# Half of the first normed rows made by ScalarE, and four of the last eight combines put ahead of the last sums

## What is computed

```python
x = x + attn_a(layernorm(x), Wv, Wg, Win, Wout, ...)   # gated, groups of 32, quadratic part and running kv sum
x = x + ffn(layernorm(x), Wr, W1, b1, W2, b2)          # 8 experts, top 2, capacity 160 per batch
x = x + attn_b(layernorm(x), q_w, k_w, v_w, l_w, ...)  # 16 heads of 64, softmax over the query axis
x = x + ffn(layernorm(x), Wr, W1, b1, W2, b2)

def layernorm(x, eps=1e-5):
    return (x - mean(x)) / sqrt(var(x) + eps)

# in ffn, for each token and each of its two experts
y_tok = y[e_flat, b_idx, pos_c] * keep * p_flat        # the answer of the slot that the token got
out = y_tok.reshape(B, T, K, C).sum(axis=2)            # its two answers are summed
```

## Time and profile before

| | |
|---|---|
| plain runs, median of 3 | 1536.02 us (1535.35 to 1537.2) |
| profiled execution, its own time | 1544.41 us |
| span of the profiled execution | 1542.6 us |
| PE busy | 1456.9 us (94%) |
| DVE, ACT, POOL busy | 1068.5 (69%), 918.2 (60%), 282.6 us (18%) |
| chain that ended last, by engine | PE 81%, DVE 9%, ACT 5% |

### The profile page before, as it was taken

One profiled execution on the slowest core, in us unless ns is written; L12 is line 12 of the kernel. 1 busy time (PEld: TensorE's weight loads), 2 busy tenths in 40 slices (PEclk: granted clock), 3 DMA queues, 4 the chain that ended last, 5 costly groups with the idle time before them and its releaser, 6 DMA issues.

```text
span 1542.6 us, 43235 instructions
## 1 busy us (share of the span) xinstructions
PE 1456.9 (94%) x18426; PEld 1010.9 (66%) x18426; DVE 1068.5 (69%) x2176; ACT 918.2 (60%) x1723; POOL 282.6 (18%) x325
## 2 busy tenths in 40 slices
PE   6999889999999999999999999999999999999956
PEld 5889774465677755657777556577775565775746
DVE  7875047787766678876666788766667887777632
ACT  4665566555666656556666566566665656666512
POOL 4156523413000031030000311300003013000170
PEclk9999999999999999999999999999999999999987
DMA  7501221111000010010000101100001011000011
GB/s 219 185 18 47 71 62 35 43 28 44 16 16 16 16 52 23 21 45 16 15 16 16 53 23 34 45 16 15 16 16 53 22 36 43 15 19 12 2 38 35
DMA packets 44302, 58.29 MB, mean 38 GB/s; under 512 B 8199, under 2 KB 32624, under 8 KB 43984
## 3 DMA queue, kind: packets, MB, share of 16 engines
q1 hardware_dynamic: 34960, 38.27, 8.9%
q0 software_dynamic: 9152, 17.26, 4.0%
HBM read 22.14 MB, written 19.32 MB: 27 GB/s over the span
## 4 chain that ended last, share of the span: by engine, by line
PE 81%; DVE 9%; ACT 5%; another core or an unknown queue 3%; issue 2%; DMA 0%; DVEq 0%; ACTq 0%; SPq 0%
PE bank L1075 28%; PE bank L1088 24%; PE bank L1003 5%; DVE nmx L1110 4%; PE bank L1008 3%; PE bank L1017 3%; PE bank L401 3%; PE bank L373 2%; ACT prob L1119 2%; PE bank L1230 2%; PE bank L1226 2%; PE bank L1187 1%; ACT hT L495 1%; PE bank L774 1%
## 5 line engine op out<-in xcount | busy, mean ns | idle before, releaser
L1119 ACT ACTIVATE prob<-bank,nmx 128x1024 f32<-128x1024 f32 x512 | 570.2, 1114 | 440.7 <-DVE nmx L1110 439.4
L1110 DVE TENSOR_REDUCE nmx<-bank 128x1 f32<-128x1024 f32 x512 | 625.8, 1223 | 211.0 <-PE bank L1075 195.8
L1088 PE MATMUL bank<-prob,vsc 64*64 64x512 f32 x4096 | 643.4, 590 | 4.7 <-DVE ctxT L1137 3.0
L1075 PE MATMUL bank<-q,k 64*64 64x512 f32 x2048 | 531.7, 593 | 14.5 <-ACT prob L1119 13.2
L1075 PE MATMUL bank<-q,ks 64*64 64x512 f32 x2048 | 529.1, 592 | 0.0
L1088 PEld LDWEIGHTS bank<-prob,vsc 64*64 64x64 f32 x4096 | 233.7, 133 | 130.2 <-issue 63.5
L1003 PE MATMUL bank<-xT,wqkv_sb 64*64 64x256 f32 (+1 forms) x1560 | 211.7, 434 | 0.0
L1075 PEld LDWEIGHTS bank<-q,ks 64*64 64x64 f32 x2048 | 135.7, 132 | 85.1 <-issue 24.2
L1647 POOL DMA_INDIRECT yg<-yslots,row_ring x64 | 65.1, 1017 | 587.1 <-PE bank L1075 571.7
L1075 PEld LDWEIGHTS bank<-q,k 64*64 64x64 f32 x2048 | 133.2, 133 | 53.9 <-ACT prob L1119 27.6
L1003 PEld LDWEIGHTS bank<-xT,wqkv_sb 64*64 64x64 f32 x1560 | 91.8, 133 | 87.7 <-issue 32.2
(11 more groups left out here) (264 smaller groups left out, 1646.1 us busy)
## 6 DMA issues: line engine op xcount, KB each, us to landing
ks<-k SPq DMA_DIRECT2D x64, 256.0 KB
yslots<-slots_sb SPq DMA_DIRECT2D x7, 640.0 KB, 3.6
slots_sb<-xslots SPq DMA_DIRECT2D x5, 640.0 KB, 4.5
xslots<-xhat_r POOLq DMA_DIRECT2D x5, 512.0 KB, 7.1
yslots<-xhat_r POOLq DMA_DIRECT2D x5, 512.0 KB, 12.2
w_sb<-in_w SPq DMA_DIRECT2D x1, 2048.0 KB, 9.4
wqkv_sb<-in_wqkv SPq DMA_DIRECT2D x1, 2048.0 KB, 18.8
xslots<-xhat_r,row_s POOLq DMA_INDIRECT x112
```

The source lines that it names most:

```text
L1075: ins = nc.tensor.matmul(bank[rows(c), SC[h][n], :], kk[r, cols(2 * j + c, HD)], qst[pi % 2][r, cols(n, HALF)], start=True, stop=True)
L1088: ins = nc.tensor.matmul(bank[rows(h), CX[n], :], vsc[s][rows(r), rows(h)], prob[g % 3][h][rows(r), cols(n, HALF)], start=(j == 0 and firs ...
L1110: nc.vector.tensor_reduce(nmx[:, 2 * s + h:2 * s + h + 1], bank[:, SC[h][0]:SC[h][0] + 2, :], mybir.AxisListType.XY, ALU.max, negate=True) ...
L1119: nc.scalar.activation(prob[g % 3][h][:].rearrange("p (n c) -> p n c", c=HALF), bank[:, SC[h][0]:SC[h][0] + 2, :], ACT.Exp, bias=nmx[:, 2 ...
```

## The change

In the head, DVE makes a `shift` for tiles 4 to 7 only (four columns) and raises `la_warm`; then it makes tiles 0 to 3 and raises `la_xhat` by two. ACT waits for `la_warm` and makes tiles 4 to 7, then raises `la_half`. PE's second turn and POOL's bias of row 0 wait for `la_half` besides. In the tail, DVE does the first four combines of k = 1 ahead of the sums, and the other four behind them; the last four gathers count on a semaphore of their own, `g_late`. SP stores the first half of batch 2 ahead of the two stores of batch 3.

```diff
--- before.py
+++ after.py
@@ bias_gpsimd
             xb = xres[:, row * T:(row + 1) * T, :]
+            if row == 0:
+                p.wait_ge(la_half, 1)
             p.wait_ge(la_xhat, 2 * (row + 1))
@@ a_turn_tensor
                 pe.wait_ge(la_xhat, 2 * row + h + 1)
+                if row == 0 and h == 1:
+                    pe.wait_ge(la_half, 1)
                 half_turned(xhat, h, bk + h).then_inc(la_tr, 1)
@@ xhat_vector
-        def xhat_vector(v, c0, b, xh, half, done):
+        def xhat_vector(v, c0, b, xh, half, done, count=1):
...
-            ins.then_inc(done, 1)
+            ins.then_inc(done, count)
@@ f_combine_vector
-            v.wait_ge(g_ga[k], 16 * T * b)
+            if b < B or k == 0:
+                v.wait_ge(g_ga[k], 16 * T * b)
+            elif tiles[0] == 0:
+                v.wait_ge(g_ga[k], 16 * (T * b - T // 2))
+            else:
+                v.wait_ge(g_late, 16 * (T // 2))
@@ sync engine
+        def store_third(sp, h):
+
+            hold(sp, g_comb, 2 * T * B - 4 * (1 - h))
+            r = slice((B - 2) * S + h * HALF, (B - 2) * S + (h + 1) * HALF)
+            sp.dma_start(out[r, :].rearrange("(t p) c -> p t c", p=P),
+                         xres[:, (B - 2) * T + 4 * h:(B - 2) * T + 4 * h + 4, :]).then_inc(stored, 16)
@@ c_gather
-                                                 bounds_check=B * SLOTS - 1, oob_is_err=False).then_inc(ga[k], 16)
+                                                 bounds_check=B * SLOTS - 1, oob_is_err=False).then_inc(
+                                                     g_late if b == B and k == 1 and t >= T // 2 else ga[k], 16)
@@ sync engine, at the end
             for h in range(2):
+                if h == 0:
+                    store_third(sp, 0)
                 hold(sp, t_res, 2 * (h + 1))
...
-            for h in range(2):
-                hold(sp, g_comb, 2 * T * B - 4 * (1 - h))
...
+            store_third(sp, 1)
             sp.wait_ge(stored, 16 * (B + 2))
@@ scalar engine, at the start
             nc.scalar.activation(wa_hi[:], wa_sb[:], ACT.Copy).then_inc(a_split, 1)
+            a.wait_ge(la_warm, 1)
+            xhat_scalar(N_MAIN[0], 0, xhat, 1, la_half)
             a.wait_ge(consts, 1)
@@ vector engine, at the start
-            for half in range(2):
-                xhat_vector(v, N_MAIN[0], 0, xhat, half, la_xhat)
+            shift_vector(v, step, N_MAIN[0] + 4, la_warm, 4)
+            xhat_vector(v, N_MAIN[0], 0, xhat, 0, la_xhat, 2)
@@ vector engine, at the end
             answers_vector(v, [2])
+            f_combine_vector(v, step, B, 1, range(T // 2))
             sums_vector(v)
-            f_combine_vector(v, step, B, 1, range(T))
+            f_combine_vector(v, step, B, 1, range(T // 2, T))
```

More of the change, by code:

```diff
@@ L154, in bass_hybrid @@
         g_ga = [sem("g_ga0"), sem("g_ga1")]
+        g_late = sem("g_late")
+        la_warm, la_half = sem("la_warm"), sem("la_half")
         t_hi, t_lo, t_oh = sem("t_hi"), sem("t_lo"), sem("t_oh")
@@ L1888, in _ @@
                              xres[:, (B - 1) * T + 4 * h:(B - 1) * T + 4 * h + 4, :]).then_inc(stored, 16)
-            for h in range(2):
-                hold(sp, g_comb, 2 * T * B - 4 * (1 - h))
-                r = slice((B - 2) * S + h * HALF, (B - 2) * S + (h + 1) * HALF)
-                sp.dma_start(out[r, :].rearrange("(t p) c -> p t c", p=P),
-                             xres[:, (B - 2) * T + 4 * h:(B - 2) * T + 4 * h + 4, :]).then_inc(stored, 16)
+            store_third(sp, 1)
             sp.wait_ge(stored, 16 * (B + 2))
```

## The result

| | before | changed |
|---|---|---|
| runs, median | 1536.83 us (1533.33 to 1539.1, 20 runs) | 1534.86 us (1532.28 to 1537.01, 20 runs) |
| profiled execution, its own time | 1544.41 us | 1535.34 us |
| its span | 1542.6 us | 1533.6 us |
| PE busy in it | 1456.9 us (94%) | 1452.4 us (95%) |

The ratio is 0.9988, with a 95% interval of 0.9983 to 0.9994: 1.8 us faster, 0.9 to 2.6. That lies above nothing and within the 0.2% that the prediction calls no change.

A forecast was written before the change was run, and what follows sets the result against it. PE, 94% busy, was taken to bound the kernel except at its two ends, where chains of waits count. Head 0.7 plus tail 1.05 gave 1.75 us off the 1536.02 median: 1534.3 us, range 1531.9 to 1537.3.

The forecast's parts named there:

- DVE's first half: Head, row 0: with the shift ahead costing 0.1 us, DVE's four tiles end at about 9.97 instead of 9.86.
- ACT's four tiles: Head, row 0: ACT makes tiles 4 to 7 in 1.64 us, unblocked by POOL, ready at 10.6 instead of 12.12.
- The chain behind: Head, after the tiles: half 1's projection begins at 14.1, and its base and lkT come 0.7 us earlier, bounds 0.4 and 1.2.
- The head's gain carried through: From the head into row 1 and on: the 0.7 us survives, with row 1's shift at about 35.2 instead of 35.93.
- The new waits: Head, POOL's and PE's queues: both waits for la_half are met at 10.6, before either engine arrives.
- The tail: End of the kernel: four combines hide in DVE's wait for PE, 0.8 us of it left; gain 1.05 us, bounds 0 and 1.1.
- The sum: Whole kernel: 0.7 + 1.05 = 1.75 us faster, 1534.3 us, 0.11%.
- The profiled time: Whole kernel: profiled execution goes from 1544.41 to 1542.7 us; plain runs are taken as 8.4 us less.
- Rival (a): Head: POOL blocks DVE's fourth tile until 11.6, projection done 0.3 to 0.8 us later than before; total 1535.3 to 1535.8; chance 0.14.
- Rival (b): PE's clock at row starts: one stretch at 1.2 GHz more or less, 1536.0 or 1532.7 us; chance 0.08 each.
- Rival (c): Last experts: one late release of ACT more, 1540 to 1545 us, or one fewer, 1523 to 1528; chance 0.06 each.
- Rival (d): Head's gain lost because a load or the zeroing ends at its own time; only the tail's remains, 1535.0 us; chance 0.04.

The follow-up runs named there:

- tail_only: The changed kernel with the head's edits undone, so only four combines stand ahead of the last sums: 1535.1 us, ratio 0.9994 against before.
- head_only: The changed kernel without its tail edits, so only ACT's making of tiles 4 to 7 of row 0 remains: 1535.38 us, ratio 0.9991 against before.
- dve_late: The changed kernel with two small DVE instructions put ahead of the head's shift, on the second chip: 1474.54 us, ratio 1.0 against before.
- no_gathers: The kernel before without POOL's last 16 gathers, a part of the computation left out, on the second chip: 1472.02 us, ratio 0.9991.
- changed_again: The changed kernel, unedited, run once more on the third chip: 1470.58 us, ratio 0.9983 against before.

## Why the prediction was right, point by point

- **DVE's first half** was to end at 9.97; it ended at 10.08. This execution had its `rstd` 0.07 later than that of before, and tiles began 0.13 later than in `tail_only`, so `shift` costs 0.13, not 0.1. PE began at 10.23 (predicted 10.1), 0.12 later than in `tail_only`.
- **ACT's four tiles** were to take 1.64 us and not to be blocked: 1.65, with POOL's subtraction beside the last two and none over 493 ns.
- **The chain behind.** The second projection began at 14.24 (predicted 14.1), the second `base` at 15.76 against 16.26. That is 0.5, at the lower part of the bounds 0.4 to 1.2, but the two executions differ in their start; against `tail_only` it is 0.8. Over all nine executions with one head or the other it is 0.3 to 0.8, so the term of 0.7 is within what was seen, at its upper part.
- **The head's gain carried through.** The prediction named `shift` of row 1 at 35.2. In this execution it stood at 36.50, later than the 35.93 of before, so this sign failed. The mechanism did not; the sign had left out when PE's products pass from a step of 0.43 to one of 0.23 us (the lower and the upper level of its clock). They passed at 16.1 in before, and at 18.1 here:

```profile
17.22 0.63 PE L737 MATMUL bank<-xT_hi,wa_lo 128*128 128x512 f32 x1
17.65 0.58 PE L738 MATMUL bank<-xT_lo,wa_hi 128*128 128x512 f32 x1
18.06 0.40 PE L736 MATMUL bank<-xT_hi,wa_hi 128*128 128x512 f32 x1
18.30 0.40 PE L737 MATMUL bank<-xT_hi,wa_lo 128*128 128x512 f32 x1
...
36.50 0.17 DVE L203 SCALAR_TENSOR_TENSOR shift<-meanvar,rstd 128x8 f32<-128x8 f32 x1
```

  Between executions that passed at the same place the gain is there: `head_only`, which passed at 15.9, has this `shift` at 35.44, 0.49 ahead of before; `tail_only`, which passed at 18.4, has it at 37.10, 0.60 behind the changed kernel.
- **The new waits** for `la_half` cost nothing: PE's eight turns follow each other without a gap.
- **The tail** was to hide four combines, leave 0.8 of the wait and give 1.05 us. It left 0.94, and from the first sum to the end there are 6.6 us instead of 7.7.
- **The sum**, 1.75 us or a ratio of 0.9989, was measured as 0.9988. That it is so close is partly luck: the interval reaches from 0.9 to 2.6 us, and the head's term alone was seen from 0.3 to 0.8. One sum of the text is off: the lower bounds of its two terms, 0.4 and 0, give 1535.6 and not 1535.3; the range holds both.
- **The profiled time.** The prediction subtracted the gain from the profiled execution (1544.41) to get 1542.7; it took 1535.34. That step was wrong in its premise, that such an execution stands 8.4 us above the plain ones: the 35 later runs of before on a chip with the same median (1536.64) all lie between 1533.17 and 1539.19. The execution that the sum was made against was an odd one, and between the two ends: its last softmax instruction of the head attention (L1119) started at 1433.70, that of `tail_only` with the same program up to there at 1426.45. The error fell out, since the same 8.4 was subtracted again.
- **Rival (a)**, the caught fourth tile, did not happen in the changed kernel, whose last tile began at 9.74. `dve_late` shows that it is real. Its place was read too late: the text has a tile held that starts behind POOL, but one that started 0.06 us ahead of POOL was held (9.88 in `tail_only`), and one 0.12 ahead was not (9.81 in `no_gathers`). So the tile at 9.78 of before was near the edge, and "the one that starts first goes on" doesn't hold by the start times of the profile. Its price was put too low: 0.3 to 0.8 later than before, where 0.9 to 1.2 was measured (17.48 against 16.57 and 16.26), of which up to 0.44 are its own added instructions.
- **Rival (b)**, a low stretch more or less, comes and goes between executions of one kernel (below). It didn't decide the result, though it may be a part of it: the 20 runs of the changed kernel have a mean clock of 0.9865, the 35 later ones of before 0.9860, and 0.0005 is some 0.4 us at the 0.8 us for 0.001 that the runs of the first chip give. **Rival (c)**, a late release more or less of 5.9 to 11 us, didn't occur. **Rival (d)**, the head's gain lost at a transfer, is spoken against by the 0.49 and 0.60 at row 1.

## What to carry to other kernels

A tile of VectorE that lasts several times its like is a reason to look at what GpSimd runs beside it; to move the GpSimd instruction by one wait brought the same place as early as to hand half of the work to a third engine did, and it is the cheaper experiment. (Over whole runs it isn't shown to be as good: the medians with POOL held were 0.9996, 1.0007 and 0.9997.) Look at the starts to 0.1 us, too: here a tile that started 0.06 us ahead of the other engine's instruction was held, and the changed kernel is free of it by about 0.1 us. Work put into a wait ahead of the last sums is free as long as its data is there on every chip that will run it, so look at when its last transfer lands, and cut the group where the wait ends. With gains of 1 us in 1500 use the timelines of the two ends for the sizes and many runs for the sign, and compare runs of the same clock: the spans of two profiled executions differed by 9 us for nothing.

## What the hardware showed beside that

**PE's clock differs between executions of one kernel.** In 13 profiled executions of 11 kernels the step of PE's first products fell from 0.43 to 0.23 us (from the lower to the upper level of its clock, 1.2 and 2.4 GHz) at any time from 15.9 to 20.5 us. In the five where it fell by 16.2, a stretch with a granted clock of about 0.5 followed, starting at 39.6 to 39.9; in the eight where it fell at 16.9 or later there was none. The changed kernel itself has been seen both ways. The chain that ended last has PE's 32 output products of row 1 in it, first of the changed kernel, then of `changed_again`:

```profile
40.60 3.57 PE bank L802 x32
```

```profile
39.64 5.20 PE bank L802 x32
```

So an early rise, which brought the `shift` of row 1 forward by a microsecond (35.54 against 36.50), was paid back 4 us behind it by 1.6 us. Such a stretch of the first profile of the changed kernel, and the time behind it (columns as in the earlier trace rows):

```profile
134.00:138.00 4.00, 4.00 (x24) 4.00 (x22) 3.21 (x15) 1.61 (x4) 1.42 (x2) 0.57 0.10 33
139.00:142.50 3.50, 3.38 (x27) 3.13 (x26) 0.91 (x2) 1.17 (x5) 2.11 (x3) 1.00 0.06 19
```

Before had six such stretches ahead of 200 us, the changed kernel three (one of them twice as long), `head_only` five (one twice as long) with the same head as the changed kernel. Their number differs as much between executions of one head as between the heads. Of the 29 runs of before on the third chip, those at a mean clock of 0.998 took 1471.05 to 1471.34 us, those at 0.991 and 0.992 1476.02 to 1476.89.

**Chips.** The same program took 1536 us on one chip and 1474 on two others. Of the 60.6 us between the spans of the changed kernel (1533.6) and of `changed_again` (1473.0), 10.7 stand at the first softmax instruction of the head attention (225.5 and 214.8), 35.5 at the last (1426.5 and 1391.0), and 25 come behind it. Part of these 25 stands in ACT's waits without a releaser in the last experts: 27 us of them on the first chip, none on the others. With them goes a low clock: PE had no product from 1480 to 1490 in the changed kernel, and was granted 0.50 from 1490 to 1500. The waits begin ahead of POOL's last 16 gathers (in the changed kernel the first ends at 1475.03 and the second begins at 1476.27, and the first gather is issued at 1479.21), and the last long one ends 1.9 us behind the issue of the last gather (1501.09 and 1499.18; 4.1 in before, 1510.62 and 1506.51). So the gathers can't have started them. Whether they lengthen them stays open, since the kernels that could tell ran where the waits do not occur.
